# Second layer's second key block made after the first layer's output products instead of before the transposes of the heads

## The reference, cut to what matters

```python
# layer 0: text = first 77 context rows, ip = the other 435, two softmaxes
q = split_heads(x @ Wq.T); k = split_heads(text @ Wk.T); v = split_heads(text @ Wv.T)
out = attend(q, k, v) + attend(q, k_ip, v_ip)
x1 = out @ Wo.T + bo + x                     # "x1": output products of the first layer
# layer 1: text = first 508 context rows, ip = the last 4
q = heads(x1 @ W_q); k_t = heads(text @ W_k); v_t = heads(text @ W_v)
probs_t = softmax(q k_t^T * scale); text_out = probs_t v_t
k_ip = heads(ip @ W_k_ip); v_ip = heads(ip @ W_v_ip)
fused = q k_ip^T * scale + 0.5 * cos(probs_t text, ip)
out = text_out + mask * softmax(fused) v_ip
y = out @ W_out + b_out + x1
```

## Time and profile before

| | us |
|---|---|
| median of 3 runs | 1626.88 |
| the runs | 1620.91, 1628.34, 1626.88 |
| profiled execution, its own time | 1620.88 |
| its span | 1619.1 |
| TensorE busy | 1521.6 (94%) |
| DVE busy | 1270.9 (78%) |
| ACT busy | 1051.9 (65%) |

### The profile page before, as it was taken

How to read it: one execution, slowest core, us unless ns; L and a number is a source line. 1 busy time by engine, 2 the same in 40 slices (tenths; PEclk the granted TensorE clock), 3 DMA queues, 4 the chain that set the end, 5 groups by cost and what they waited for, 6 DMA issues and landing times.

```text
span 1619.1 us, 24966 instructions
## 1 busy us (share of the span) xinstructions
PE 1521.6 (94%) x7536; PEld 1154.4 (71%) x7536; DVE 1270.9 (78%) x3537; ACT 1051.9 (65%) x2243; POOL 421.7 (26%) x993
## 2 busy tenths in 40 slices
PE   6899999999999999999999999999999999999993
PEld 3565389999656549999856637999965654899991
DVE  2598379998779738999779945999977983799985
ACT  1598267776269737777529936777725982777760
POOL 0244022222034302322104412222302440232220
PEclk9899999999999999999999999999999999999996
DMA  9211321111411132111131123111140113111110
GB/s 300 62 45 22 107 58 21 21 21 23 127 26 43 44 95 63 25 21 17 47 103 40 36 76 101 21 21 21 19 136 16 45 37 107 16 26 21 21 18 16
DMA packets 160222, 84.50 MB, mean 52 GB/s; under 512 B 121925, under 2 KB 130901, under 8 KB 160089
## 3 DMA queue, kind: packets, MB, share of 16 engines
q1 hardware_dynamic: 157448, 77.80, 19.5%
q10 hardware_dynamic: 2640, 5.11, 0.9%
HBM read 41.78 MB, written 34.10 MB: 47 GB/s over the span
## 4 chain that ended last, share of the span: by engine, by line
PE 85%; ACT 6%; issue 3%; SPq 2%; DVE 2%; DMA 1%; DVEq 0%; ACTq 0%
PE ps_w L1029 50%; PE ps_s L1029 16%; PE ps_t L1029 12%; PE ps_b L1029 5%; ACT probs L591 3%; PE ps_b L1154 2%; ACT probsT_high L572 1%; ACT probsT L580 1%; DMA slots<-out_all 1%; DVE row_max L802 1%; SPq L373 1%; SPq L325 0%; DMA slots<-probsT_low 0%; ACT probs L677 0%; PE ps_m L1029 0%
## 5 line engine op out<-in xcount | busy, mean ns | idle before, releaser
L572 ACT ACTIVATE probsT_high<-ps_t 128x512 fp32r<-128x512 f32 x640 | 385.1, 602 | 95.9 <-PE ps_t L1029 92.7
L787 DVE TENSOR_TENSOR probsT_low<-probsT,probsT_high 128x512 fp32r<-128x512 f32 x560 | 378.9, 686 | 17.3 <-ACT probsT L580 12.0
L580 ACT ACTIVATE probsT<-ps_t 128x512 f32<-128x512 f32 x640 | 388.2, 606 | 0.0
L1029 PE MATMUL ps_w<-gram,probsT_high 128*128 128x416 f32 (+2 forms) x1280 | 383.9, 310 | 1.1 <-issue 1.1
L1029 PE MATMUL ps_w<-gram_low,probsT_high 128*128 128x384 f32 (+2 forms) x1280 | 351.5, 303 | 0.0
L606 ACT ACTIVATE probs<-ps_s,row_max 128x508 f32<-128x508 f32 x320 | 222.5, 696 | 145.9 <-DVE row_max L852 105.5
L1029 PE MATMUL ps_s<-slots 96*128 96x512 f32 x640 | 280.6, 481 | 23.9 <-DVE row_max L802 9.3
L1029 PE MATMUL ps_t<-slots 98*128 98x512 f32 x640 | 251.6, 413 | 1.1 <-ACT probsT L580 0.2
L1029 PEld LDWEIGHTS ps_w<-gram_low,probsT_high 128*128 128x128 f32 (+1 forms) x1280 | 241.9, 189 | 6.3
L1029 PE MATMUL ps_w<-gram,probsT_low 128*128 128x400 f32 (+2 forms) x1280 | 245.9, 314 | 0.0
L1029 PEld LDWEIGHTS ps_w<-gram,probsT_high 128*128 128x128 f32 (+1 forms) x1280 | 240.4, 188 | 6.1 <-issue 1.8
(11 more groups left out here) (175 smaller groups left out, 1854.1 us busy)
## 6 DMA issues: line engine op xcount, KB each, us to landing
slots<-parts SPq DMA_DIRECT2D x128, 192.0 KB, 3.4
slots<-row_max SPq DMA_DIRECT2D x640, 0.5 KB, 2.0
parts<-probsT_high SPq DMA_DIRECT2D x16, 512.0 KB, 4.2
parts<-probsT_high SPq DMA_DIRECT2D x24, 256.0 KB, 4.1
parts<-probsT_low SPq DMA_DIRECT2D x8, 512.0 KB, 3.6
parts<-x_sb SPq DMA_DIRECT2D x8, 512.0 KB, 3.9
slots<-probsT_high SPq DMA_DIRECT2D x24, 128.0 KB, 3.3
parts<-probsT_low SPq DMA_DIRECT2D x12, 256.0 KB, 3.6
```

Source lines behind the costliest of these rows:

```text
L572: nc.scalar.activation(probsT_high[1 - par][:, t, :], ps_t[:, t % 2, :], ACT.Exp, scale=scale)
L580: nc.scalar.activation(probsT[:, t, :], ps_t[:, t % 2, :], ACT.Exp, scale=scale).then_inc(pt_block[l], 1)
L787: nc.vector.tensor_tensor(probsT_low[1 - par][:, t, :], probsT[:, t, :], probsT_high[1 - par][:, t, :].bitcast(F32), ALU.subtract).then_in ...
L1029: return nc.tensor.matmul(out, lhsT, rhs, start=start, stop=stop)
```

## The change

Block 1 of `k1` leaves its place behind block 0 and goes between `x1` and `q1`, in `JOBS` (and with that in the ring of banks) and on TensorE, ACT and DVE. SP's order stays as it was.

```diff
 JOBS = (
-    [("k1", m, "D") for m in range(KEYS1)]
+    [("k1", 0, "D")]
     + [("tr0", m, "A") for m in range(CBN)]
     + [("x1", m, "D") for m in range(CBN)]
+    + [("k1", 1, "D")]
     + [("q1", m, "D") for m in range(CBN)]
...
-                highs(b, "k1")
+                high(b, "k1", 0)
                 move_transposed(b, "tr0")
+                high(b, "k1", 1)
                 highs(b, "q1")
...
-                lows(b, "k1")
+                low(b, "k1", 0)
                 dve.wait_ge(y_out, 16 * CBN * b + 16)
                 for m in range(CBN):
                     wait_job(dve, b, "x1", m)
...
+                low(b, "k1", 1)
                 lows(b, "q1")
...
-                keys(b, "k1", "ki1", TEXT1, range(KEYS1))
+                keys(b, "k1", "ki1", TEXT1, (0,))
                 transposed_heads(b, "tr0", 0)
                 wait_freed(pe, b, "tr0", CBN - 1)
                 by_channels(b, "x1", "o0", heads_outT)
+                keys(b, "k1", "ki1", TEXT1, (1,))
                 wait_freed(pe, b, "x1", CBN - 1)
                 by_channels(b, "q1", "q1", x1_sb)
```

## The result

The changed kernel takes 1634.3 us in the median of 20 runs (1626.03 to 1637.16), the kernel before 1626.45 in 20 runs (1620.17 to 1628.34). The ratio is 1.0045, with a 95% interval from 1.0033 to 1.0057: slower by 0.45%, or some 7.3 us (the two medians lie 7.9 us apart). The forecast was 1636.0, in a range from 1626 to 1641. The profiled execution of the changed kernel has a span of 1632.6 us, against 1619.1. That is 13.5 us, more than the medians differ, because the profiled execution of the kernel before was one of its fastest.

What follows compares the result with a forecast made beforehand. TensorE, busy 94% of the span, was taken as the bound; order +4.86 and clock falls +4.2 made +9.1 us, which with the runs' median 6.0 above the profiled 1620.88 gave 1636.0 us, range 1626 to 1641.

Steps and rivals of the forecast that it cites:

- The cover at the transposes: Before the transposes, batches 1 to 3: without key block 1 TensorE idles 2.74 us for DVE's normalisation; transposes start 0.89 earlier.
- The late place, +2.79: Between x1 and the queries, all batches: key block 1 adds 3.62 us, hides the 0.83 wait, so costs 2.79.
- The order's sum, +4.86: Joints between the layers, order alone: +1.90 us in each of batches 1 to 3, -0.84 in batch 0.
- What stands behind: From the queries on: everything shifts along, nothing is given back; key block 1's stores against query loads taken as 0.
- The second rival: First scores of layer 1: stores of key block 1 delay query loads, 0.6 us a batch, +2.4 on top; chance 0.14.
- the fourth: Behind the queries: loads or a wait in layer 1 swallow the shift, so 0 change, 1626.9 us; chance 0.05.
- The third, heads never late: At the transposes: normalisation ends before key block 0 in all batches, each gaining 0.84 us, -3.4 in all; chance 0.03.
- The clock, +4.2: Joints of batches 1 to 3: idling drops TensorE's clock in all three, 1.4 us a fall, bounds 0 and 5.1.
- The comparison with the passages behind layer 1: Clock fell in two of three passages idling 1.7 in 2.5 us; 3.5 idle in 5.0 should bring falls in all three joints.
- the sign that the first block of `x1` would take over 3.5 us: Changed profile, batches 1 to 3: low clock would stretch the first x1 block from 2.9 to over 3.5 us.
- The sign against the forecast, a clock that stays at 1.00: Joints of batches 1 to 3: a granted clock staying at 1.00 would show the forecast wrong.
- The first rival: Joints of batches 1 to 3: clock holds or falls only once, +4.9 to +6.3 us, 1631.8 to 1633.2; chance 0.28.

Runs made afterwards that it cites:

- The late block alone: Kernel before plus four matmul calls with unused results between x1 and the queries in all four batches; 1631.59 us, ratio 1.0047.
- the gap filled: Changed kernel plus three matmul calls with unused results between key block 0 and the transposes in batches 1 to 3; 1628.79 us, ratio 1.0022.

## Why the prediction was right, and where it was not

**The cover at the transposes: right.** From the end of key block 0 in the earlier trace rows the idle time was forecast at 2.74; it is 2.69 in batches 1 to 3 and none in batch 0. The experiment with the shorter normalisation shows that DVE's chain sets it.

**The late place, +2.79: right.** From x1 to the queries the changed kernel takes 12.44 us in batch 1 (567.14 to 579.58), forecast 12.49. The late block alone shows this price by itself.

**The order's sum, +4.86: right.** Without the falls the four joints are +4.95 against before: 1.95 in each of batches 1 to 3 and -0.88 in batch 0, up to rounding (forecast 1.90 and -0.84). The waits of TensorE, 8.1 us in place of 3.3, say the same. The cleaned means give +4.2 for the changed kernel and +5.0 with the gap filled.

**What stands behind: right.** The stores of key block 1 don't delay the first loads; the idle time ahead of the first scores is 0.24 to 0.27 in every profile. The second rival, +0.6 a joint, is out. So is the fourth: the shift isn't swallowed. The third, heads never late, holds in batch 0 alone, where the gain of 0.88 came.

**The clock, +4.2: the direction right, the reasoning half right.** The step that failed is "I expect the clock to fall in all three". It falls in 5 of 15, so in the mean once a run, and this makes 3 x 5/15 x 1.20 = +1.2 in the joints. The comparison with the passages behind layer 1, more idling and therefore more falls, was wrong: the new gap, 2.69 us idle and 0.77 behind the transposes, brought falls less often (5 of 15) than 0.23 and 1.47 us there (21 of 27 over both kernels). The price of a fall was taken at 1.4 and is 1.20, the lower bound, which came from the transposes at low clock in the earlier trace rows: the clock falls on the transposes or ahead of them and is back at x1. So the sign that the first block of x1 would take over 3.5 us didn't come; it takes 3.04. The sign against the forecast, a clock that stays at 1.00, came in 10 of the 15 joints. What I had held to be the same in both kernels, the passages, brings the rest: 13 falls in 15 against 8 in 12 are 0.6 more in a run, at some 1.5 us +0.9. So 4.95 + 1.2 + 0.9 = 7.1 us, against 7.9 between the medians and an interval from 5.4 to 9.3. Two more stages vary with the clock, the image products (+0.7 in the mean of the profiles) and the end of the program (-0.5); with five profiles against four it can't be told whether the change moves them. The total of the forecast, +9.1, is high by the falls that didn't come. That it lies so near the result is in part luck: falls in the passages, which weren't in the sum, make up for some of those that were. And where the forecast set 0.55 on slower by over 0.5%, the measured 0.45% lies on the other side of that line, with an interval (0.33 to 0.57) that takes in both. The first rival (the clock holds or falls once, +4.9 to +6.3) describes the joints (+6.2) better than the forecast did.

Open is why the clock falls at one passage and not at another with the same gaps, and so whether a kernel of another length would meet the same.

## What to carry to other kernels

Independent work in front of a wait is worth the length of the wait, as far as the work is long enough, and behind it the length of the next one: compare the two gaps (2.7 and 0.83 us here) before moving a block, in each repetition on its own, since the first can differ from the rest. Where a block is longer than either gap, cut it, in a bank of its own: the same products then took 3.6 us less in the joints than before, 0.22%. And a gap on TensorE can cost more than its length, through the clock (1.20 us in 5 of 15 joints here). To judge the order by itself, compare the stretches of several profiles between the same markers, those with a fall and those without apart: total times hold falls at other places too. Or fill the gap with work whose result is thrown away, as above, and measure that kernel.

## What the runs showed of the hardware

Two things were not expected. First, the clock also fell in a stretch in which TensorE showed no idle time: during the image products (32 instructions, 24 of them with 16 moving columns) it went to 1.2 GHz in 8 of 9 profiles of the two kernels, and they then take 7.9 to 8.3 us instead of 4.98. In the changed kernel's first profile they begin so:

```profile
159.61 0.44 PE L1157 MATMUL ps_b<-ident,probs 68*128 68x68 f32 x4 [0.77 <-ACT probs L592]
159.88 2.86 PE L1032 MATMUL ps_m<-root,w_ki 128*128 128x16 f32 x16
```

TensorE had idled 0.51 and 0.77 us just ahead of them, in the profile without a fall as in those with one. Whether those gaps or the small products bring the fall, no run separates. Second, the falls repeat: the same passage behaved alike in nearly all executions of a kernel (behind batches 0, 1 and 2 the clock fell in 4, 0 and 4 of 4 before, and in 3, 5 and 5 of 5 after the change). So the falls aren't chance alone, and a change in one place can bring a fall in another whose own work and gap are the same as before.
